# A mixture-of-experts block on one core: routing, tile slots and row sending are moved between the steps

## What is computed

```python
x0 = zX * lap_x(x) + zY * lap_y(x) + zR * x * (1 - x)      # one row of 256 numbers is a token
qkv = layernorm1(x0) @ in_proj_w.T + in_proj_b
probs = softmax(causal(q @ k.T / 4))                       # 16 heads of 16, over the 16 images
x1 = x0 + (probs @ v) @ out_proj_w.T + out_proj_b
hn2 = layernorm2(x1)
rp = softmax(hn2 @ router_w.T)                             # 8 experts, the best two count
y = sum over the two best e: rp[e] * gelu(hn2 @ w1[e]) @ w2[e]     # w1: 256 x 512, w2: 512 x 256
return x + x1 + y
```

## Time and profile before

| what | us |
|---|---|
| three runs, median (lowest to highest) | 716.42 (716.0 to 716.69) |
| the profiled execution: span from its first to its last instruction | 715.1 |
| of it PE busy | 588.2 (82%) |
| POOL busy | 464.4 (65%) |
| DVE busy | 434.7 (61%) |
| ACT busy | 349.2 (49%) |

### The profile page before, as it was taken

How to read it: one execution, slowest core, us unless ns; L and a number is a source line. 1 busy time by engine, 2 the same in 40 slices (tenths; PEclk the granted TensorE clock), 3 DMA queues, 4 the chain that set the end, 5 groups by cost and what they waited for, 6 DMA issues and landing times. The chain is left out here.

```text
span 715.1 us, 10162 instructions
## 1 busy us (share of the span) xinstructions
PE 588.2 (82%) x2640; PEld 409.1 (57%) x2640; DVE 434.7 (61%) x1028; ACT 349.2 (49%) x814; POOL 464.4 (65%) x562
## 2 busy tenths in 40 slices
PE   2667786777679877889997899988699999999992
PEld 1334454554456645656665566666467766766761
DVE  1266689879999999655977799969735000111110
ACT  4434443334335544438674466645346555444440
POOL 5787677797697538666678865864585843434432
PEclk9779997867579989889999799999999999999997
DMA  4367864222122214313333313343344544443342
GB/s 127 125 224 225 252 162 103 62 71 48 42 64 69 46 31 86 69 42 67 68 82 66 78 23 69 68 83 54 68 91 80 119 71 73 67 68 61 69 53 22
DMA packets 51547, 59.83 MB, mean 84 GB/s; under 512 B 7386, under 2 KB 47075, under 8 KB 51428
## 3 DMA queue, kind: packets, MB, share of 16 engines
q0 software_dynamic: 18288, 23.28, 20.4%
q1 hardware_dynamic: 33204, 35.91, 17.7%
HBM read 35.89 MB, written 27.46 MB: 89 GB/s over the span
## 5 line engine op out<-in xcount | busy, mean ns | idle before, releaser
L982 PE MATMUL b_y<-w_s,hm_hmT 128*128 x568 | 138.0, 387 | 11.5 <-ACT y L551 10.8
L967 PE MATMUL b_h<-w_s,xT 128*128 x284 | 135.2, 599 | 1.6 <-ACT xT L512 1.6
L449 POOL DMA_INDIRECT out_dram<-y,xin x71 | 119.5, 1683 | 26.1 <-issue 21.9
L982 PEld LDWEIGHTS b_y<-w_s,hm_hmT 128*128 128x128 f32 x568 | 104.1, 193 | 25.8 <-issue 14.3
L1119 PE MATMUL b_at<-ident,pv_prod 128*128 128x128 f32 x544 | 79.0, 298 | 23.8 <-DVE pv_prod L913 23.8
L913 DVE TENSOR_TENSOR pv_prod<-kv,pr 128x1024 f32<-128x1024 f32 (+2 forms) x80 | 85.0, 1105 | 21.1 <-PE b_at L1119 20.9
L684 DVE TENSOR_SCALAR y<-b_y,xin,live 128x256 f32<-128x256 f32 x24 | 13.1, 544 | 137.2 <-PE b_y L982 137.2
L847 DVE TENSOR_TENSOR qk_prod<-q,kv 128x1024 f32<-128x1024 f32 (+2 forms) x80 | 89.2, 1139 | 2.6 <-ACT kv L581 1.8
L1119 PEld LDWEIGHTS b_at<-ident,pv_prod 128*128 128x128 f32 x544 | 70.2, 158 | 27.7 <-issue 22.0
L414 POOL DMA_INDIRECT xs_d<-ring,slot_row x64 | 71.2, 1112 | 18.7 <-issue 18.1
L855 DVE TENSOR_REDUCE sc<-qk_prod 128x64 f32<-128x1024 f32 (+2 forms) x80 | 82.1, 1051 | 0.3
(11 more groups left out here) (168 smaller groups left out, 1026.1 us busy)
## 6 DMA issues: line engine op xcount, KB each, us to landing
xin<-xs_d SPq DMA_DIRECT2D x71, 132.5 KB, 2.2
w_s<-in_L_ffn_w_dram SPq DMA_DIRECT2D x16, 512.0 KB, 4.2
xp<-in_x_dram SPq DMA_DIRECT2D x32, 128.0 KB
xud<-in_x_dram SPq DMA_DIRECT2D x32, 128.0 KB
out_dram<-x POOLq DMA_DIRECT2D x32, 128.0 KB, 3.2
xud<-in_x_dram SPq DMA_DIRECT2D x32, 126.0 KB
out_dram<-y,xin POOLq DMA_INDIRECT x71
xud<-in_x_dram SPq DMA_DIRECT2D x64, 1.0 KB
```

The source lines that it names most:

```text
L449: pool.indirect_dma_start(out_rows, bass.IndirectOffsetOnAxis(ap=xin[:, j % NX, H:H + 1].bitcast(U32), axis=0), y[:, j % NY, :], None, com ...
L967: mm = pe.matmul(b_h[:, :], xT[:, k * P:(k + 1) * P], w1_s[:, bass.ds(e * (HC * F) + k * F, F)], start=(k == 0), stop=(k == HC - 1))
L982: mm = pe.matmul(b_y[:, 0:H], hmT[:, k * P:(k + 1) * P], w2_s[:, bass.ds(e * (FC * H) + k * H, H)], start=(k == 0), stop=(k == FC - 1))
```

## The change

The routing moves, the tiles' pipeline is planned part by part, and the loading of tiles is asked for by need.

- `ROUTE` is one step earlier: three steps after a group's last one. The logits of that last step are those that TensorE makes in this very step, so `top` and `top_index` of them move to the end of the step, before `route_a`.
- `route_b` is split. `route_slots` (the weights and slots) now stands in the middle of the next step, before the value products; `route_tiles` (the table of tiles) stays at its end.
- The rows of a group are sent in two steps where it took up to three: one of its steps at the end of the step in which the slots are made, two at the beginning of the next and two at its end (`SPOTS`).
- A slot is now four numbers (a, b, c, d): `turn_in` of a, `up` of b, `turn_h` and `down` of c, the result of d. Each may be none. At the end of a group's tiles the pipeline runs out (b, c and d go on without a new a), and the next group's first `turn_in` may come in the step right after its last rows have been sent.
- SP loads what a slot of a needs, up to tile a + 1, and at a step's beginning the tile of the next slot; a tile of a group is asked for at the earliest in the step after its last rows were sent (`in_rows_from`).
- `WANT` has two slots from step 10 on, where it had them from step 13.

```diff
-        ROUTE = {GROUPS[r][-1] + 4: r for r in range(NG - 1)}
-        PER = 2
+        ROUTE = {GROUPS[r][-1] + 3: r for r in range(NG - 1)}
+        SPOTS = ((1, 1), (2, 0), (2, 0), (2, 1), (2, 1))
         for g, r in ROUTE.items():
-            for i, step in enumerate(GROUPS[r]):
-                SCATTER[g + 2 + i // PER, i % PER] = step
+            for (later, n), step in zip(SPOTS, GROUPS[r]):
+                SCATTER.setdefault((g + later, n), []).append(step)
...
-        WANT = [0] * 13 + [2] * 7 + [1] * 2 + [2] * 10 + [1] * 3
+        WANT = [0] * 10 + [2] * 10 + [1] * 2 + [2] * 10 + [1] * 3
...
+        def next_slot(g):
+            a = turned if turned < ALL and in_rows_from(turned) <= g else None
+            b = raised if raised < turned else None
+            c = lowered if lowered < raised else None
+            d = given if given < lowered else None
+            return a, b, c, d
...
-            def slot(j):
-                if j == -1:
-                    tile_in(0)
-                    tile_in(1)
-                if j + 3 < ALL:
-                    tile_in(j + 3)
+            def ask(g, n):
+                while asked[0] < min(n, ALL) and in_rows_from(asked[0]) <= g:
+                    tile_in(asked[0])
+                    asked[0] += 1
+            def slot(g, a):
+                if a is not None:
+                    ask(g, a + 2)
...
-                    ordered = top(g - 4) if 0 <= g - 4 else None
+                    ordered = top(g - 4) if 0 <= g - 4 and g - 1 not in ROUTE else None
...
+                    if g - 1 in ROUTE:
+                        route_slots(ROUTE[g - 1])
                     for m in range(NPIECE[v]):
                         value_products(m)
...
-                    route_a(ROUTE[g], last)
+                    route_a(ROUTE[g], top_index(top(g - 3)))
                 if g - 1 in ROUTE:
-                    route_b(ROUTE[g - 1])
+                    route_tiles(ROUTE[g - 1])
...
-            left = [j - 1 for j in done_in(G + 2)] + list(range(LEFT[0] - 1, ALL))
-            while left[0] < LEFT[1]:
+            left = given_in(G + 2) + list(range(IN_LOOP, ALL))
+            while left[0] < IN_LOOP + 2:
                 add_y(left.pop(0))
             for g in GROUPS[NG - 1]:
                 scatter(g)
```

More of the change, by code:

```diff
@@ L228, in runs, with given_in @@
             return out
-        def done_in(g):
-            return [j for n in range(NPLACES) for j in SLOTS.get((g, n), ()) if j >= 1]
+        def given_in(g):
+            return [d for n in range(NPLACES) for a, b, c, d in SLOTS.get((g, n), ()) if d is not None]
         def added_to(j):
@@ L335, in _ @@
                     copy_x((g + 1) // 2)
+                if g >= 0:
+                    ask(g, [a for i in range(g, G + 3) for n in range(NPLACES) for a, b, c, d in SLOTS[i, n] if a is not None][0] + 1
+                        if any(a is not None for i in range(g, G + 3) for n in range(NPLACES) for a, b, c, d in SLOTS[i, n]) else 0)
                 for n in range(NPLACES):
-                    place(g, n)
-            for j in LEFT:
-                slot(j)
+                    for a, b, c, d in SLOTS[g, n]:
+                        slot(g, a)
+            for a, b, c, d in LEFT:
+                slot(G + 3, a)
             for i in range(NCOPY):
@@ L552, in result, with slot @@
                                scale=xin[:, j % NX, bass.ds(e + (H + 1), 1)]).then_inc(s["y_sb"], 1)
[L554 to L564, removed]
+            def slot(a, b, c, d):
+                if c is not None:
+                    turned_h(c)
+                if d is not None and d < TAIL:
+                    result(d)
+                if b is not None:
+                    gelu(b)
+                if a is not None:
+                    turned_in(a)
             def place(g, n):
-                for j in SLOTS[g, n]:
-                    slot(j)
+                for a, b, c, d in SLOTS[g, n]:
+                    slot(a, b, c, d)
             def exponentials(g):
@@ L613, in _ @@
                     odds(ROUTE[g - 1])
-                if g >= 0 and SLOTS[g, 0] and g < G:
+                if 0 <= g < G and any(b is not None for n in range(NPLACES) for a, b, c, d in SLOTS[g, n]):
                     act.activation(junk[:, 0:1], junk[:, 1:2], ACT.Gelu)
@@ L637, in _ @@
                     place(g, n)
-            slot(LEFT[0])
+            slot(*LEFT[0])
             odds(NG - 1)
-            for j in LEFT[1:]:
-                slot(j)
+            for a, b, c, d in LEFT[1:]:
+                slot(a, b, c, d)
         @block.vector
@@ L991, in _, with slot @@
             loaded = {}
-            def slot(j):
-                if j == -1:
+            def slot(a, b, c):
+                if a == 0:
                     pe.wait_ge(s["w1_in"], 16 * E)
                     pe.wait_ge(s["w2_in"], 16 * E)
[L997 to L1009, removed]
+                if b is not None:
+                    loaded[b] = next_expert(b)
+                if c is not None:
+                    turn_h(c)
+                if b is not None:
+                    up(b, loaded[b])
+                if a is not None:
+                    turn_in(a, a % NX, a // NX + 1)
+                if c is not None:
+                    down(c, loaded.pop(c))
             def router(g):
@@ L1020, in place @@
             def place(g, n):
-                for j in SLOTS[g, n]:
-                    slot(j)
+                for a, b, c, d in SLOTS[g, n]:
+                    slot(a, b, c)
             def count_tokens(r):
```

44 lines of the change are left out of this document (25 added, 19 removed).

## The result

The changed kernel takes 738.73 us in the median (736.96 to 741.0, 4 runs), beside 716.21 us (715.96 to 716.69) for the kernel before: a ratio of 1.0318, with a 95% interval of 1.0292 to 1.0344. That is 22.5 us slower, where the forecast was 9.7 us faster; the miss is 32.0 us. The profiled execution has a span of 738.5 us.

The account below looks back on a forecast made before the run. VectorE bounds steps 10 to 15, both engines are near full in steps 26 to 31, TensorE bounds the tail. Terms sum to -9.7 us on a 715.1 us span; with 1.3 us carried over, 706.7 us, range 690 to 722.

Parts of the forecast that it names:

- Choosing at the end of the own step: Six choosing steps: `top` waits for logits made in the same step; +2 us, between 0 and 6 x 2.2.
- A group's first tile just in time: Steps 10, 14, 18, 23, 28: TensorE waits for a tile load just issued; +5 us, between 0 and 28.
- the 15 that the prediction named as its sign of being wrong: Whole kernel: waits for the tile load of over 15 us in all would show the prediction wrong.
- the rival on the other side: Steps 14, 18, 23, 28: first tile's 7.0 us wait paid in full, 729.7 us; decides from 14.7 us; chance 0.17.
- The rival in which everything is covered: Loop: waits fall into TensorE's idle time and the loop ends as before; 689.7 us; chance 0.22.
- Step 25 (0): Step 25, without slots before, takes two tiles at no cost, its 18.7 us not being TensorE's; 0 us.
- the tail (-28.7): After the loop: 33 tiles left in place of 40, seven fewer at 4.1 us each; -28.7 us.
- Steps 10 to 15: These steps take more tile work, covered by TensorE's idle time beside VectorE; +4 us, between 0 and 7.8.
- POOL's larger bites: Up to six row DMAs, not four, before deviations VectorE waits for, at six places; +6 us, between 0 and 16.
- The last group's rows: After the loop: TensorE waits for tile 47, whose rows are sent late; +4 us, between 0 and 4.9.
- Rows out of steps 32 and 33: Steps 32 and 33: rows that held up a deviation are gone; -2 us, between -4 and 0.
- The rival of the low clock: Steps 10 to 15: the new tile work runs wholly at 1.2 GHz; 718.7 us; chance 0.06.

Follow-up runs that it names:

- by other data: Changed kernel, last step of the first six groups routed by the step before's logits: 722.73 us; four first tiles reading earlier rows: 729.60; both: 718.37.
- by order: Changed kernel with experts chosen one step later: 718.48 us; with a group's tiles turned one step later: 721.40 us; both: 714.05 us.
- the kernel of 709.82 us: Changed kernel with choosing and first tile each a step later, plus rows sent over one half step more and later tile loads: 709.82 us.
- two pairs of kernels: Rows spread, loads later: with choosing and first tile a step later, 714.05 to 709.82 us; with only first tile a step later, 721.40 to 715.66.

## Why the prediction was wrong

*Choosing at the end of the own step (+2, upper end 13): the step that failed first.* It measured 16.0 us by other data and 20.3 by order in the changed kernel, and 14.9 alone in the kernel before. I priced six groups by one row, that of step 20, and even six times its 0.7 us would be 4.2. It was right for step 20 (0.70) and too high for step 29 (none); steps 7, 11, 15 and 25 had 4.35 to 9.35 us. Step 20 is the one with tiles whose slot stands behind the logits, and in step 29 VectorE came late. The upper end counted only the tile work in front of the router, not the rest of TensorE's step.

*A group's first tile just in time (+5, upper end 28).* I let the wait disappear in steps 10 and 14 "in TensorE's idle time". But behind it on TensorE's queue stands the projection for which VectorE waits, 5.56 us in step 11, and the idle time of an engine that another waits for is no cover. The waits came to 32.3 us, above the 15 that the prediction named as its sign of being wrong; 26.4 of them stand at the five first tiles (6.64, 6.92, 2.01, 2.83 and 7.97 us in steps 10, 14, 18, 23 and 28), and the two that I took for covered are among the longest. A step's delay for the tiles gave back 17.3 us, but 4.4 once the choosing was out of the way. This was also the rival on the other side (729.7 us): its mechanism was at work and its point of decision, 14.7 us, was passed (19.7 in its four steps), but the loss was only partly its own. The rival in which everything is covered fell with the loop's end at 583.9.

*Step 25 (0) and the tail (-28.7).* The tail's 4.1 us for each tile was right. Step 25 took its two tiles as forecast once the waits were taken away (19.0 us, against 18.7 empty; in the changed kernel, with its wait for logits, 23.4), and yet they won nothing: 4.5 us came back in steps 21 to 33, and the tail was only 2.3 us shorter for them, since without them its gap in front of tile 47 is covered. "Its 18.7 us were not TensorE's" was true, but the earlier trace rows also had steps 26 to 31 with both engines near full; that TensorE used step 25 to catch up is likely, and not shown apart from the waits.

*Steps 10 to 15 (+4, upper end 7.8).* In the changed kernel +24.3, past the 8 us that the prediction named as its other sign of being wrong. With neither wait in them they took 4.1 us more than before in the kernel of 709.82 us, but for three finished tiles in place of five. What the five would cost there without waits was not run.

*POOL's larger bites (+6):* 4.2 and 5.7 us in two pairs of kernels, which also differ in when the loads are asked for. The size is near, but by luck as far as the runs show: the price was for VectorE's waits for a deviation, and these rose from 20.9 to 21.8 us in all. Behind six row DMAs they did appear in three of the six places (3.02, 2.21 and 0.46 us, none there before), but about as much went elsewhere, and spreading the rows did not lower the total (25.6 to 25.8 and 18.7 to 32.1). What fell was TensorE's wait for the tile load (13.4 to 5.9, 6.9 to 5.2) and, in the second pair, VectorE's for the output projection (43.8 to 31.8). How the bites cost their time stays open. *The last group's rows (+4, upper end 4.9):* the gap in front of tile 47 was 3.72 us as expected, but cost 6.9 (last section). *Rows out of steps 32 and 33 (-2):* 0.8 us less by the starts of VectorE's steps (18.0 against 18.8), 2.6 from the start of step 32 to the loop's last `down` (23.0 against 25.6).

The prediction also read the slices of the earlier trace rows too smoothly (VectorE at 8 and 7 in slices 7 and 8, TensorE at 7 and 6 in slices 21 and 28); none of its sums rests on that.

These do not simply add up to the 32.0 us, as the two waits are links of one chain (16.0 and 9.1 alone, 20.4 together by data; 20.3, 17.3 and 24.7 by order). What is settled is that both waits cost time, that rows sent in smaller bites with later loads save some, and that the tiles of step 25 come back as delay; how the last few us divide among them is open.

## What to carry over

A wait that an edit adds should be priced at each place where it will stand, by what the engine it waits for still has queued in front of the awaited instruction, not by one row from one place. Idle time of one engine covers new work only if nobody waits for what is queued behind that work; here three tiles, later and without a wait for their load, cost 4.1 us in steps 10 to 15, where they cost 12.3 after the loop. When routing and rows are to come earlier, work out the slots in mid-step, send rows in small bites (what these spare is open), and leave the choosing where its logits have long been there: 709.8 us.

## What was not expected of the hardware

A wait cost TensorE more than its length. Timeline of the changed kernel in step 28 and at tile 47, and windows of the wait for tile 47 and of what follows (columns as in the earlier trace rows):

```profile
493.63 0.69 PE L982 MATMUL b_x<-ident,xin 128*128 128x128 f32 x2 [7.97 <-DMA xin<-xs_d]
494.11 3.62 PE L1006 MATMUL b_y<-w_s,hm_hmT 128*128 x8
...
613.71 1.88 PE L991 MATMUL b_h<-w_s,xT 128*128 x4
...
619.31 0.69 PE L982 MATMUL b_x<-ident,xin 128*128 128x128 f32 x2 [3.72 <-DMA xin<-xs_d]
...
619.79 3.62 PE L1006 MATMUL b_y<-w_s,hm_hmT 128*128 x8
...
624.06 2.37 PE L991 MATMUL b_h<-w_s,xT 128*128 x4
```

```profile
615.00:619.30 4.30, 0.59 (x2) 0.00 (x0) 0.00 (x0) 0.70 (x2) 3.33 (x3) 0.87 0.49 91
619.30:624.00 4.70, 4.69 (x14) 3.87 (x15) 0.00 (x0) 0.81 (x2) 0.00 (x0) 0.50 0.53 114
```

After 3.72 us without work the granted clock was 0.50, 1.2 GHz, for the next 4.7 us, and `down` took 3.62 us where it takes 1.89 in the same timeline at full clock. So a gap of 3.72 us cost 6.9 (the tail's 142.2 us less 33 tiles at 4.1). The same followed the wait of step 28 (7.97 us, then `down` at 3.62). In step 10 the clock was low already ahead of the wait (0.58 from 133.0 to 137.7, where `b_qk` took 3.62 us), so the slow `up` of tile 0 there (3.78 us) cannot be put down to the wait alone. The rival of the low clock was right that it would cost something, and it was right about tile 0 in step 10; for steps 10 to 15 as a whole it was not, as they had 0.80, above the 0.73 of the earlier trace rows.

The Trainium skill, TensorE: Matmul & The Clock Gate, section "What's actually happening", says that the throttled state is the default and activity releases it; these rows agree. I had used that rule only for work that gets denser, and not for the gaps that the change makes.
